# Routing a mixture of experts: logits from the output product, choices by max and index, slot lists of two kinds, a table of weights

## What is computed

```python
x = layernorm(x + attention(x, Wqkv, bqkv, Wout, bout))
logits = x @ router_w.T + router_b
w = softmax(logits)                          # 8 experts
topk_flat = w kept at its 2 largest, else 0
expert_mask = topk_flat > 0
sorted_indices = argsort(-expert_mask, axis=0)[:512]   # the first 512 tokens of each expert
out_e = relu(x[idx_e] @ W1_e) @ W2_e * w[idx_e, e]     # 7 experts, 256 -> 1024 -> 256
combined = scatter-add of out_e at idx_e
combined = combined + x * w_noop                       # if the no-op was among the two
x = layernorm(x + combined)
```

## Time and profile before

| | us |
|---|---|
| median of 3 runs | 1193.81 |
| lowest, highest | 1191.54, 1195.57 |
| the profiled execution | 1199.86 |
| its span, first to last instruction | 1197.8 |

### The profile page before, as it was taken

The page is one execution under the profiler, slowest core; times in us unless marked ns, Lnnn a source line. Parts: engine busy times, 40 slices in busy tenths (PEclk is TensorE's granted clock), DMA queues, the critical chain, the costliest instruction groups (busy, mean ns, idle before and its releaser), DMA issues. The chain is left out here.

```text
span 1197.8 us, 35440 instructions
## 1 busy us (share of the span) xinstructions
PE 1078.7 (90%) x15545; PEld 689.9 (58%) x15545; DVE 441.4 (37%) x951; ACT 811.3 (68%) x779; POOL 278.8 (23%) x415
## 2 busy tenths in 40 slices
PE   7999699999999999998999999999596389999990
PEld 3555465557656565755557656555485356666650
DVE  4677234444224232252344324222544711111115
ACT  3554699999999999997999999999134411111115
POOL 2333022112211111122212211111530233333220
PEclk9999799999999999999999999999887689999995
DMA  6645212222121111123212121100621414444317
GB/s 206 208 157 175 72 38 78 67 58 62 54 61 54 44 45 40 41 79 106 73 54 69 46 68 51 39 12 6 221 85 53 144 49 110 106 109 107 89 21 285
DMA packets 74478, 103.15 MB, mean 86 GB/s; under 512 B 11089, under 2 KB 61137, under 8 KB 74321
## 3 DMA queue, kind: packets, MB, share of 16 engines
q1 hardware_dynamic: 64384, 88.29, 23.6%
q0 software_dynamic: 5376, 7.34, 3.5%
q10 hardware_dynamic: 4560, 5.19, 1.4%
HBM read 65.83 MB, written 30.77 MB: 81 GB/s over the span
## 5 line engine op out<-in xcount | busy, mean ns | idle before, releaser
L822 ACT ACTIVATE prob<-ps 128x1536 f32<-128x1536 f32 (+4 forms) x504 | 667.4, 1461 | 40.3 <-PE ps L778 38.8
L778 PE MATMUL ps<-q_stack,k_stack 111*32 111x512 bf16 (+17 forms) x6848 | 431.8, 312 | 21.5 <-SPq L303 8.0
L802 PE MATMUL ps<-prob,v_head 128*32 128x128 f32 (+7 forms) x7228 | 431.4, 340 | 0.0
L778 PEld LDWEIGHTS ps<-q_stack,k_stack 111*32 111x32 bf16 (+5 forms) x6848 | 216.8, 97 | 209.4 <-ACT prob L822 113.2
L802 PEld LDWEIGHTS ps<-prob,v_head 128*32 128x32 f32 x7228 | 243.4, 110 | 78.1 <-issue 17.5
L833 POOL TENSOR_TENSOR prob<-prob,near_bias 128x128 f32<-128x128 f32 x256 | 125.7, 495 | 572.9 <-ACT prob L822 572.6
L833 DVE TENSOR_TENSOR prob<-prob,near_bias 128x128 f32<-128x128 f32 x256 | 79.3, 317 | 458.0 <-ACT prob L822 457.9
L1629 ACT ACTIVATE hT<-ps 128x512 f32<-128x512 f32 x28 | 16.7, 597 | 152.6 <-PE ps L1592 152.6
L851 DVE RECIPROCAL o_rec<-o_den 128x128 f32<-128x128 f32 x128 | 113.0, 923 | 0.6
L1592 PE MATMUL ps<-xeT,w 128*128 128x512 f32 x224 | 99.3, 602 | 0.7 <-ACT xeT L1622 0.7
L1604 PE MATMUL ps<-w,hT 128*128 128x256 f32 x448 | 97.8, 379 | 0.0
(11 more groups left out here) (145 smaller groups left out, 597.4 us busy)
## 6 DMA issues: line engine op xcount, KB each, us to landing
qk_parts<-split SPq DMA_DIRECT2D x32, 384.0 KB, 3.2
w<-L_ffn_experts_inter_dram SPq DMA_DIRECT2D x7, 1024.0 KB, 6.2
w<-n_L_ffn_experts_out_dram SPq DMA_DIRECT2D x7, 1024.0 KB, 10.0
q_stack<-qk_parts SPq DMA_DIRECT2D x31, 192.0 KB
k_stack<-qk_parts SPq DMA_DIRECT2D x31, 192.0 KB
xin<-in_L_attn_x_dram ACTq DMA_DIRECT2D x8, 512.0 KB, 4.0
heads<-o_out SPq DMA_DIRECT2D x128, 32.0 KB, 2.4
v<-in_L_attn_x_dram SPq DMA_DIRECT2D x8, 512.0 KB, 5.3
```

The lines of the kernel that those rows point to most:

```text
L778: mm = pe.matmul(ps[k:k + keys, SLOT_BANKS * (c % 2) + bank, col:col + z - a], k_st[n % STACKS][0:rows, kb * P + k:kb * P + k + keys], q_s ...
L802: mm = pe.matmul(ps[32 * g:32 * g + 32, 6 + n % 2, column:column + width * times], vh[n % 2][:, kb, :], moving, start=g not in begun, stop ...
L822: act.activation(prob[:, c % RING, 0:at + z - a], ps[:, bank:bank + SLOT_BANKS, :].rearrange("p c n -> p (c n)")[:, 0:at + z - a], ACT.Exp ...
```

## The change

**The router logits come out of the output product.** The layer norm is linear up to its scale, so logits = (y @ centred router) x 1/std + bias. `w_qkv` and `w_out` get 9 extra columns (`EXTRA`: 8 for the experts, 1 for the minus mean). For that, PE turns the router and the output weights in chunk 0 (`turn_weights`), and `extra_columns` multiplies them; DVE first centres the router's rows. The v tile gets rows of 265, and the attention output product writes 265 columns, one bank per tile. The v product of the projection also gets one bank per tile, 6 and 7 in turn. Transposes, logit products and normalised rows of the routing are gone.

**Rows are stored as z with 1/std and shift in two more columns** (`z_rows`, 258 wide); ACT normalises them after the gather (`normalise_rows`). The statistics are ACT's: the sum of squares by `Square` with `accum_out`.

**Choices** by `max` (eight largest, sorted) and `max_index`, one of each per tile; the mask is taken from a gap of logits instead of a weight.

**Lots of two kinds** (tile plus one, token) instead of six, 4 x 7 x 32 columns with the tokens innermost; slot and slot tile are computed for each pick (32 columns) rather than for each expert (256); the counting products are bf16.

**A table of weights**: softmax and the weights of the picks are computed at the start of the expert block, stored as `token_weights` (4096 rows of 8), and gathered per slot by POOL (`gather_weights`). The running sums' first value moves into expert 0's block too (`keep_rows`).

**Moved**: POOL adds the output bias during attention (`add_bias` at the chunks `BIAS_AT` = 361, 364, 367, 370 and 485, 488, 491, 494; chunk 485 is the first of the last head), and `load_rows` of batch 1 goes ahead of the last two heads' stores.

```diff
+EXTRA = E + 1
+DX = D + EXTRA
+ROW = D + 2
+BIAS_AT = [FIRST[-8] + 3 * c for c in range(QG)] + [FIRST[-1] + 3 * c for c in range(QG)]
@@ project_phase, sync
-            load_route_weights(sp, t, wout, bout, router_w, router_b)
+            sp.wait_ge(router_set, 1)
+            sp.dma_start(router[0:E, :], router_w).then_inc(router_in, 16)
+            sp.dma_start(t["w_out"][:, :, 0:D], wout.rearrange("(k p) n -> p k n", p=P)).then_inc(w_out_in, 16)
...
+            load_route_weights(sp, t, bout, router_b)
@@ project_phase, tensor
             def v_product(i, par, pair):
-                pe.wait_ge(v_done, i * 4 + par * 2 + pair + 1)
-                for s in range(2):
-                    tok = (pair * 2 + s) * P
+                for s in range(pair * 2, pair * 2 + 2):
+                    pe.wait_ge(v_done, (i * 2 + par) * TPC + s + 1)
                     for k in range(2):
-                        mm = pe.matmul(ps[:, 6 + pair, s * D:(s + 1) * D], xT[par][:, k, tok:tok + P],
-                                       w[:, k, 2 * D:3 * D], start=(k == 0), stop=(k == 1))
-                mm.then_inc(v_mm, 1)
+                        mm = pe.matmul(ps[:, 6 + s % 2, 0:DX], xT[par][:, k, s * P:(s + 1) * P],
+                                       w[:, k, 2 * D:3 * D + EXTRA], start=(k == 0), stop=(k == 1))
+                    mm.then_inc(v_mm, 1)
...
                 qk(i, par)
+                if n == 0:
+                    turn_weights()
+                    transposes(i + par, 1 - par)
+                    extra_columns()
                 v_product(i, par, 0)
@@ project_phase, vector
+            dve.wait_ge(router_in, 16)
+            dve.tensor_reduce(router_mean[:, :], router[0:E, :], AX.X, ALU.add).then_inc(router_done, 1)
...
             def add_v(i, par, pair):
-                dve.wait_ge(v_mm, i * 4 + par * 2 + pair + 5)
-                dve.tensor_tensor(t["v"][:, bass.ds((i * 2 + par) * TPC + pair * 2, 2), :],
-                                  ps[:, 6 + pair, :].rearrange("p (s n) -> p s n", s=2), bv[:, :, :],
-                                  ALU.add).then_inc(v_done, 1)
+                for s in range(pair * 2, pair * 2 + 2):
+                    tile = (i * 2 + par) * TPC + s
+                    dve.wait_ge(v_mm, tile + 9)
+                    dve.tensor_tensor(t["v"][:, tile, :], ps[:, 6 + s % 2, 0:DX], bv[:, :], ALU.add).then_inc(v_done, 1)
@@ attention_phase
             for n in range(len(ITEMS) - STACKS, len(ITEMS)):
+                if n == len(ITEMS) - 2:
+                    sp.wait_ge(vh_done, len(ITEMS))
+                    load_rows(sp, 1)
                 store_turned_heads(n)
-            sp.wait_ge(vh_done, len(ITEMS))
-            load_rows(sp, 1)
...
                 near_blocks(pool, c, 1, diag_odd)
+                if c in BIAS_AT:
+                    add_bias(pool, BIAS_AT.index(c))
@@ route_phase, tensor
+            for n in range(NCH):
                 if n >= 2:
-                    pe.wait_ge(lg_done, n - 1)
+                    pe.wait_ge(z_done, n - 1)
+                    pe.wait_ge(extra_done, n - 1)
                 for s in range(TPC):
+                    tok = n * CH + s * P
                     for k in range(2):
+                        mm = pe.matmul(ps[:, n % 2 * TPC + s, 0:DX], heads[:, k, tok:tok + P], wo[:, k, :],
+                                       start=(k == 0), stop=(k == 1))
+                mm.then_inc(y_mm, 1)
@@ route_phase, scalar
+                for s in range(TPC):
+                    act.activation(unused[:, s, :], z[:, n * TPC + s, 0:D], ACT.Square, bias=extra[n % 2][:, s, E:EXTRA],
+                                   accum_out=squares[n % 2][:, s:s + 1]).then_inc(sq_done, 1)
@@ route_phase, vector
+                for at in range(n * TPC, (n + 1) * TPC):
+                    dve.max(best[:, at, :], logits[:, at, :]).then_inc(best_done, 1)
+                dve.wait_ge(best_done, (n + 1) * TPC)
+                for at in range(n * TPC, (n + 1) * TPC):
+                    dve.max_index(order[:, at, :], best[:, at, :], logits[:, at, :]).then_inc(order_done, 1)
...
+            for k in range(PICKS):
+                for what in range(2):
+                    dve.tensor_tensor(lots[k][:, what, :, :, :],
+                                      lot_of[what][:, k, :, :].rearrange("p a (e t) -> p a e t", e=1)
+                                      .broadcast_to([P, ST, EX, NT]),
+                                      picks[:, k, 0:EX, :].rearrange("p (a e) t -> p a e t", a=1)
+                                      .broadcast_to([P, ST, EX, NT]), ALU.mult).then_inc(lots_done, 1)
@@ expert_phase, scalar
+                def normalise_rows(e, s):
+                    rows = xe[e % 2][:, s, :]
+                    act.wait_ge(xe_in[e % 2][s], 16 * (e // 2 + 1))
+                    act.activation(rows[:, 0:D], rows[:, 0:D], ACT.Identity, bias=rows[:, D + 1:ROW],
+                                   scale=rows[:, D:D + 1]).then_inc(xe_done, 1)
...
                     for j in range(0, FT, 2):
                         act.wait_ge(up_mm, e * FT + j + 1)
                         act.activation(hT[:, j, :], ps[:, 2, :], ACT.Relu).then_inc(h_done[0], 1)
+                        if e == 0:
+                            keep_rows(j // 2)
+                        elif e + 1 < EX:
+                            normalise_rows(e + 1, j // 2)
...
                 for e in range(EX):
                     relu(e)
+                    if e == 0:
+                        for s in range(ST):
+                            normalise_rows(1, s)
                     if e + 1 < EX:
                         evacuate(e + 1)
+                    if e == 0:
+                        for n in range(FT // 2, NCH):
+                            keep_rows(n)
@@ expert_phase, gpsimd
                 for e in range(2):
                     gather(e)
+                pool.wait_ge(weights_out, 16)
+                for e in range(2):
+                    gather_weights(e)
                 for e in range(EX):
                     if e + 2 < EX:
                         gather(e + 2)
                     add(e)
+                    if e + 2 < EX:
+                        gather_weights(e + 2)
```

More of the change, by code:

```diff
@@ L1108, in route_phase @@
+        heads, z, best, picks = t["heads"], t["v"], t["best"], t["picks"]
+        extra = [sb(f"extra{p}", [P, TPC, EXTRA], F32) for p in range(2)]
+        squares = [sb(f"squares{p}", [P, TPC], F32) for p in range(2)]
         sd = [sb(f"std{p}", [P, TPC], F32) for p in range(2)]
[L1109 to L1110 removed]
+        unused = sb("unused", [P, TPC, D], F32)
         eps = sb("eps", [P, 1], F32)
@@ new lines, in route_phase @@
+        order = sb("best_experts", [P, NT, E], U32)
+        gap = sb("gap", [P, NT], F32)
+        mask = sb("mask", [P, E, NT], BF16)
+        so_far = sb("so_far", [P, E, NT], BF16)
+        of_pick = sb("earlier_of_pick", [P, PICKS, E, NT], F32)
+        slot = sb("slot", [P, PICKS, NT], F32)
+        of_tile = sb("slot_tile", [P, PICKS, NT], F32)
+        place = sb("slot_place", [P, PICKS, NT], BF16)
+        in_tile = sb("in_slot_tile", [P, PICKS, ST, NT], BF16)
+        lot_of = [sb(f"lot_{what}", [P, PICKS, ST, NT], BF16) for what in ("tile", "token")]
@@ L1283, in root @@
                 if n >= 2:
                     act.wait_ge(rs_done, n - 1)
-                act.activation(sd[n % 2][:, :], mv[n % 2][:, :, 1], ACT.Sqrt, bias=eps[:, 0:1]).then_inc(sd_done, 1)
-            def normalise(n):
-                act.wait_ge(shift_done, n + 1)
-                for s in range(TPC):
-                    rows = x1[:, n * TPC + s, :]
-                    act.activation(rows, rows, ACT.Identity, bias=shift[n % 2][:, s:s + 1],
-                                   scale=rstd[n % 2][:, s:s + 1]).then_inc(ln_done, 1)
@@ L1409, in _ @@
+            count[0] += 2
+            dve.wait_ge(step, count[0])
+            link(dve.scalar_tensor_tensor(out=picks[:, 1, :, :],
+                                          in0=gap[:, :].rearrange("p (e t) -> p e t", e=1).broadcast_to([P, E, NT]),
+                                          scalar=-GONE, in1=picks[:, 1, :, :], op0=ALU.is_gt, op1=ALU.mult))
+            dve.tensor_tensor(mask[:, :, :], picks[:, 0, :, :], picks[:, 1, :, :], ALU.add).then_inc(mask_done, 1)
             dve.wait_ge(mask_done, 1)
@@ new lines, in _ @@
+            link(dve.tensor_tensor(of_pick[:, :, :, :], before, picks[:, :, :, :], ALU.mult))
+            link(dve.tensor_reduce(slot[:, :, :], of_pick[:, :, :, :].rearrange("p k e t -> p k t e"), AX.X, ALU.max))
+            link(dve.tensor_scalar(of_tile[:, :, :], slot[:, :, :], float(P), None, ALU.is_ge))
+            for n in range(2, ST + 1):
+                link(dve.scalar_tensor_tensor(out=of_tile[:, :, :], in0=slot[:, :, :], scalar=float(n * P),
+                                              in1=of_tile[:, :, :], op0=ALU.is_ge, op1=ALU.add))
```

617 lines of the change are left out of this document (304 added, 313 removed).

## The result

The changed kernel takes 1163.3 us (median of 4 runs, 1160.5 to 1163.7) against 1194.7 for the kernel before on the same chip (4 runs, 1191.5 to 1195.7): a ratio of 0.9737, 95% interval 0.9712 to 0.9761. The forecast was 1169.0 (1156 to 1188). The profiled execution took 1162.99, its span is 1161.3, 36.5 less than that of the profile before; by the medians the gain is 31.4. The forecast gain was 24.8.

What follows compares the result with a forecast made beforehand. It took TensorE to bound most stages and DVE the slot lists. Terms -29.6 - 15.6 + 0.3 + 4.6 + 16 - 0.5 = -24.8 us, from the median 1193.81 to 1169.0 us, range 1156 to 1188.

Steps and rivals of the forecast that it cites:

- projection: Projection stage: value tiles wait for DVE's sums in two banks, 2.0 us a chunk; +16 us in total, bounds +5 and +28.
- Chunk 0: Projection's first chunk: turning weights, extra columns, the router mean and a stretch at 1.2 GHz cost +8.0 us.
- The six chunks: Projection's following chunks: waits, DVE's shift widening and half clock make 91.2 us of 83.2, +8.0.
- Rival 1: Projection: each added wait also drops PE to 1.2 GHz, +12 us, about 1183 in all; chance 0.12.
- Rival 2: Projection hides the added waits and the lots run at the fast rate: 13 us less, 1156; chance 0.10.
- Rival 5: Slot lists stay long because PE's products end them: 4 us less gained, 1173; shares the forecast's 0.64.
- Output product: Output product stage: PE bounds it at 3.83 us a chunk, 39.0 us instead of 68.6, -29.6.
- Rival 4: Output product: DVE's max and max_index bound it from 0.17 us each; chance 0.07 at 0.2 to 0.4 us, 0.03 beyond.
- Rival 3: Output product: ACT bounds it through two table loads a chunk, 1181 us in all; chance 0.03.
- Slot lists: Lists of slots: everything hangs on DVE, 17.4 us instead of 33.0, -15.6, bounds -18 and -12.
- Start and expert 0: Expert stage: start +0.3 us; in expert 0 transposes wait for ACT's normalise steps, +3.0 plus 1.6 at 1.2 GHz, +4.6.
- Attention: Attention: POOL's eight bias sums just hidden, 0 (bounds 0 and +4); four loads fewer behind the last head, -0.5 us.

Runs made afterwards that it cites:

- the second profile of before: The kernel before, unchanged, run again for another profiled execution: 1194.6 us, one run.
- three more profiles of this code: Profiles of three edits of the changed kernel with its order in expert 0: value sums ahead of low parts 1156.9 us, max twice 1165.4, weights' store later 1163.2.
- The two-bank edit of before: The kernel before, with one bank per value tile, two in all, and DVE adding the bias tile by tile: 1202.5 us, ratio 1.0064.
- the longer wait: The changed kernel with two unread 128x512 subtractions ahead of DVE's first value sum in every projection chunk but the first: 1178.4 us, one run.
- the faster kernels: Edits of the changed kernel, among them value sums ahead of low parts, 1156.9 us; with three further edits 1148.0; with the shift's widening also moved 1146.8.
- the doubled kernel: The changed kernel with every max and max_index of the output product done twice, the second time into unread tiles: 1165.4 us, one run.
- three such moves of order: In the changed kernel: value sums ahead of low parts, 1156.9 us; expert 1's rows ahead of running sum, 1159.2; chunk 0 reordered, with both and later weights' store, 1148.0.

## Why the prediction was right or wrong

The sign and the order of the terms were right, and the time lay inside the range; the forecast gain of 24.8 us was 6.6 too small by the medians. Most of the miss is the projection, forecast dearer than it is. Against the second profile of before (the first lay 5 us above its median, as the prediction allowed for in its last step):

| term | forecast | measured |
|---|---|---|
| projection | +16 | +11.5 (+8.2 against the recorded profile; over the four profiles with this projection +8.2 to +14.2) |
| attention and its end | -0.5 | -1.4 |
| output product, lists, start of experts | -44.9 | -46.8 |
| expert 0 and after | +4.6 | +5.5 (+2.1 to +2.8 in three more profiles of this code) |

**Projection.** The wait was read rightly: its place, its releaser, its 2.0 us (1.92 alone in the kernel before). Three terms were too large or left out, and against the second profile of before they make up the 4.5 us between +16 and +11.5.

*Chunk 0*, forecast +8.0, measured +6.7. The second q/k product starts at 31.45, 33.02, 32.95 and 32.99 us in four profiles of kernels with this projection, before at 25.61 and 24.79. Much of the spread is the length of the very first product, 8.64 to 10.12 us. Without it the starts are 22.8 to 23.0 and 15.5 us, so the term itself is +7.3 to +7.6.

*The six chunks*, forecast 91.2 us, measured 88.1. The half clock behind the widened shift (1.6) came in one of the four profiles only, a chunk takes 14.34 and not 14.53 us, and the shift adds 2.1 and not 2.4. Against the 81.5 of the second profile this is +6.6 for +8.0, against the recorded one +4.9.

*The stage's end*, forecast at nothing. From the last q/k product to attention it takes 18.5 us (17.9 to 18.8 in the other three), before 21.1 and 20.3, though the work is longer. SyncE's last four stores of parts, in the kernel before (first row) and in the changed one:

```profile
114.86 6.44 SPq L385 DMA_DIRECT2D qk_parts<-split  x4
125.66 4.41 SPq L404 DMA_DIRECT2D qk_parts<-split  x4
```

With longer chunks SyncE is done with the stack loads 2.4 us behind the start of the last q/k product, before 6.0 and 4.9, and these stores are issued in 4.41 us instead of 6.44 and 5.63. The two-bank edit of before shows that the slower chunks alone shorten the end (17.7), the longer wait shortens it further (16.8), and the faster kernels give it back (19.4 to 20.5). That SyncE's queue is the reason is read from these rows; no run moves its stores alone. The prediction's sentence "The stage's end, the last stores of parts, follows these chunks" was the mistake: it is 1.7 to 2.6 us.

**Rival 1** (0.12) fell: behind the waits of 1.60 us the rest of the value product took 2.05 to 2.06 us in every chunk of the four profiles. The longer wait shows how near it was: with 1.33 us more the clock falls in five of six chunks. **Rival 2** gave 1156 for hidden waits; the waits were not hidden. **Rival 5** fell too: the lists took 17.2 us.

**Output product.** 36.1 us for 39.0. PE's cycle is 3.58, not 3.83: the prediction scaled the busy time of 3.70 for 16 instructions, which overlaps the next ones; the starts of product and transposes lie 3.53 apart in the kernel before, and 3.53 x 265/256 = 3.65:

```profile
887.63 3.70 PE L1229 MATMUL ps<-w_out,heads 128*128 128x256 f32 x16
891.16 1.04 PE L1239 MATMUL ps<-ident,v 128*128 128x128 f32 x8
```

The cycle of 3.58 for 3.83 is 1.8 of the 2.9 us; the last chunk's chain was 5.7, not 6.4. Max and max_index cost 0.105 to 0.13 each, taken at 0.1. **Rival 4** would have needed 0.17 to begin by the prediction's sum, and 0.21 by the 0.62 us that DVE is idle in a chunk; the doubled kernel, with 1.05 + 0.84 us or 0.24 for each of the eight, is past that point and 0.22 a chunk slower. **Rival 3** is refuted: there is no table load between Square and the root. The Trainium skill, "ScalarE: Activation LUTs", Table sets, says that a load comes with a switch of sets; by that rule and this trace, Square is in the set that holds the root.

**Slot lists.** 17.2 for 17.4, ended by DVE's wait of 1.77 for PE's last group (forecast 1.9). The lots of 896 run at 0.62 us, the fast rate.

**Start and expert 0.** The start was 0.9 us dearer than the 0.3 forecast (11.67 us from the block's first DVE instruction to the first up product, before 10.49). The prediction named small pieces of the weights' store delaying the row gathers as a thing that would make it wrong, and gave it no price; without the store in the way it is 10.65, so 1.0 us is that. The store itself was done early by far: the gathers of weights began at 923.08 without a wait, so the store, issued at 915.08, took at most 8 us, not 14. Expert 0's stall was forecast at 3.0 plus 1.6 for the half clock. In the changed kernel's profile the down product starts 4.0 instead of 0.7 us behind the up product's end, it takes 15.02 instead of 13.98, and the up product 16.97 instead of 15.93: 3.3, 1.0 and 1.0. In the three more profiles of this code the stall is 2.8 and neither product is longer than before, 13.98 and 15.5 to 15.8. So the wait was sized well (2.8 for 3.0), the half clock behind it is not the rule, and that +5.5 lies near +4.6 is luck. The sum rows' stores did not hold ACT ahead of the stall.

**Attention.** POOL waited 3.53 us for batch 1's rows and its near block came at 823.14, 6.1 behind the copy at 817.08; forecast was 7.3 (818.5 against 811.17). DVE's last product of the stage starts 34.88 us behind that copy in both kernels (817.08 to 851.96, 811.17 to 846.05): just hidden, as said. The 1.4 us less can't be put down to the change: nine profiles with this attention have 718.7 to 720.7 us, the two of before 722.6 and 721.2, but the two edits of before, which leave attention as it was, 721.3 (two banks) and 718.1 (router loads moved). The -0.5 of the forecast can't be told either.

## What to carry to other kernels

A wait that is added where a queue is already the late one replaces a wait instead of adding to it, and the queue's own stretch at the stage's end shortens: look for who is late at the end before the wait is multiplied by the number of chunks. For the pace of a pipelined engine take start to start, not the busy time of the group. Where a helper engine serves two, put the step that frees a bank ahead of the one that feeds a store: three such moves of order (value sums, expert 1's rows, chunk 0) gave 15 us, half as much as the whole change. And compare several profiles of the same code before a term is called confirmed: one execution had a half clock in expert 0 that three others didn't.

## What the runs showed of the hardware

- A stop of PE of 1.60 us in every 14.3 was never followed by the lower clock in four profiles (2.05 us for the rest of the product each time); a stop of 2.93 was followed by 1.2 GHz in five of six chunks (2.77 to 3.90 us). A stop of 2.0 to 2.4 ahead of a q/k product was followed by it in some executions (8.73 to 8.80 us for the product) and not in others (7.10 to 7.11).
- POOL can stop DVE: while POOL added 128x1024 (L798, 2.18 to 2.19 us), three of DVE's near blocks of 128x128, otherwise 0.29 us, took 1.89, 2.05 and 1.02:

```profile
821.01 2.18 POOL L798 TENSOR_TENSOR v<-v,b_out 128x1024 f32<-128x1024 f32 x1 [3.53 <-DMA v<-in_L_attn_x_dram]
821.45 1.89 DVE L917 TENSOR_TENSOR prob<-prob,near_bias 128x128 f32<-128x128 f32 x1 [2.68 <-ACT prob L906]
...
824.40 2.05 DVE L917 TENSOR_TENSOR prob<-prob,near_bias 128x128 f32<-128x128 f32 x1 [1.06 <-ACT prob L906]
```

Each of the three ends 0.15 to 0.16 us after POOL's sum does (823.34 behind 823.19, 826.45 behind 826.29 for the sum from 824.11, 833.18 behind 833.03), so DVE stood until POOL was done. A shuffle of one input (128x512, from 827.09) beside another of these sums took 0.73 us, as without one (0.72). POOL's sum was no longer for it. The Trainium skill, "SBUF — State Buffer", says in "SBUF: two separate sides" that the port pair which the two engines share is an exclusive lock, held for the whole instruction, and that a DVE instruction with two SBUF inputs needs it when a GpSimd operation reads SBUF; these rows agree.
- A Square with its sum read out costs ACT 0.49 us a tile of 256: the read of the accumulator (0.18 to 0.19) runs beside the Squares and adds nothing to that pitch.
